# A graph layer's edge loop: two VectorE rows and one ScalarE row of each pair of edge tiles take another place

## The reference, cut to what matters

```python
x_cat = jnp.concatenate([node_feat[src], node_feat[dst], edge_feat], axis=-1)
r = x_cat @ Wr.T + br
q = (node_feat @ Wq.T + bq).reshape(n, H, D)
k = (r @ Wk.T + bk).reshape(e, H, D)
v = (r @ Wv.T + bv).reshape(e, H, D)
a = jnp.einsum('ehd,ehd->eh', q[dst], k) * scaler
amax = jax.ops.segment_max(a, dst, num_segments=n)
ae = jnp.exp(a - amax[dst])
asum = jax.ops.segment_sum(ae, dst, num_segments=n)
m = v * (ae / asum[dst])[..., None]
out = jax.ops.segment_sum(m, dst, num_segments=n).reshape(n, H * D)
```

## Time and profile before

| what | value |
|---|---|
| time, median of 3 runs | 1842.91 us |
| the profiled execution's own time | 1842.91 us |
| its span, first to last instruction | 1841.1 us |
| PE busy | 1623.5 us (88%) |
| DVE busy | 1296.4 us (70%) |
| ACT busy | 1026.3 us (56%) |
| POOL busy | 697.5 us (38%) |

### The profile page before, as it was taken

How to read it: one execution, slowest core, us unless ns; L and a number is a source line. 1 busy time by engine, 2 the same in 40 slices (tenths; PEclk the granted TensorE clock), 3 DMA queues, 4 the chain that set the end, 5 groups by cost and what they waited for, 6 DMA issues and landing times. The chain is left out here.

```text
span 1841.1 us, 26829 instructions
## 1 busy us (share of the span) xinstructions
PE 1623.5 (88%) x7162; PEld 1189.9 (65%) x7162; DVE 1296.4 (70%) x3259; ACT 1026.3 (56%) x3674; POOL 697.5 (38%) x723
## 2 busy tenths in 40 slices
PE   7989979999999999999999999999993777888523
PEld 6867767777777777777777777777772333444311
DVE  5875728887888878887888788878883455322688
ACT  3882225777677777777777767776773344100011
POOL 0001224555555555555555555555551000000033
PEclk9999989999999999999999999999995888999855
DMA  5664327566666666666666666666653324000001
GB/s 181 205 227 154 124 86 238 194 207 212 208 205 201 216 211 207 199 217 212 210 201 212 213 216 199 213 215 201 214 161 130 128 88 137 0 1 0 23 12 44
DMA packets 129670, 300.28 MB, mean 163 GB/s; under 512 B 29088, under 2 KB 50727, under 8 KB 129522
## 3 DMA queue, kind: packets, MB, share of 16 engines
q0 software_dynamic: 63600, 180.17, 29.1%
q1 hardware_dynamic: 60738, 107.59, 19.4%
q10 hardware_dynamic: 5184, 10.81, 1.6%
HBM read 271.40 MB, written 66.58 MB: 184 GB/s over the span
## 5 line engine op out<-in xcount | busy, mean ns | idle before, releaser
L1196 ACT ACTIVATE wv<-vv,expd 128x64 f32<-128x64 f32 x1256 | 316.6, 334 | 2.8
L1208 ACT ACTIVATE old<-old,expd 128x64 f32<-128x64 f32 x1256 | 307.7, 334 | 0.0
L1140 POOL DMA_INDIRECT merge<-new,put_id x157 | 161.1, 1026 | 273.7 <-DVE new L1366 242.1
L1409 PE MATMUL psK<-M_hi,efT_hi 128*128 128x512 f32 x628 | 253.4, 403 | 6.4 <-ACT efT_hi L1166 6.4
L1409 PE MATMUL psV<-M_hi,efT_hi 128*128 128x512 f32 x628 | 255.9, 408 | 0.0
L1410 PE MATMUL psV<-M_lo,efT_hi 128*128 128x512 f32 x628 | 249.7, 398 | 0.0
L1410 PE MATMUL psK<-M_lo,efT_hi 128*128 128x512 f32 x628 | 249.2, 397 | 0.0
L1111 POOL DMA_INDIRECT old<-merge,dst_id x157 | 156.0, 994 | 138.3 <-DMA merge<-new,put_id 112.6
L1111 POOL DMA_INDIRECT kv<-kv_table,src_id x157 | 157.1, 1001 | 72.7 <-issue 47.8
L1182 ACT ACTIVATE expd<-diff 128x32 f32<-128x32 f32 (+1 forms) x79 | 18.1, 229 | 293.9 <-DVE diff L1347 293.9
L1111 POOL DMA_INDIRECT qc<-q_table,dst_id x157 | 155.6, 991 | 53.0 <-issue 46.9
(11 more groups left out here) (271 smaller groups left out, 3404.6 us busy)
## 6 DMA issues: line engine op xcount, KB each, us to landing
efT<-in_ef_turned_dram SPq DMA_DIRECT2D x78, 512.0 KB, 5.0
merge<-empty ACTq DMA_DIRECT2D x4, 2640.0 KB, 9.7
rows<-merge SPq DMA_DIRECT2D x40, 264.0 KB, 3.7
row_block<-dst_rows POOLq DMA_DIRECT2D x13, 768.0 KB, 5.8
dst_line<-dst_rows SPq DMA_DIRECT2D x78, 128.0 KB, 2.7
end_line<-end_rows SPq DMA_DIRECT2D x78, 128.0 KB, 4.1
kv_table<-kv_out SPq DMA_DIRECT2D x10, 512.0 KB, 3.2
raw<-in_L_gnn_Wr_dram SPq DMA_DIRECT2D x12, 256.0 KB, 5.1
```

The lines of the kernel that those rows point to most:

```text
L1140: pool.indirect_dma_start(out=merge[2 * (p % 2) + u][:, :], out_offset=bass.IndirectOffsetOnAxis(ap=put_id[:, t:t + 1], axis=0), in_=new[p ...
L1196: act.activation(wv[:, u, h * DH:(h + 1) * DH], vv[p % 2][:, u, h * DH:(h + 1) * DH], ACT.Copy, scale=expd[p % 2][:, u, 0, h:h + 1]).then_ ...
L1208: act.activation(rows, rows, ACT.Copy, scale=expd[p % 2][:, u, 1, h:h + 1]).then_inc(old_scaled, 1)
L1409: pe.matmul(out[:, :], efT_hi[b][:, u, c, :], Me_hi[:, c, col:col + D], start=c == 0, stop=False)
```

## The change

ACT: the rounding of the weights (`exp_hi`) was issued as the last step of a round, behind `weigh_v`. It now stands right behind the exponential. DVE: `exp_lo` and the first `wv_lo` stood behind the scan. They now stand between the two `vv`. The second `wv_lo` stood between the scores of the two tiles and now stands ahead of both. No instruction is added or taken out.

```diff
@@ scalar: weights(p) @@
                 act.activation(expd[p % 2][:, 0:n, :, :], diff[p % 2][:, 0:n, :, :], ACT.Exp, scale=SCALE).then_inc(exp_ready, 1)
-
-            def weights_high(p):
-                n = tiles_of(p)
                 act.wait_ge(exp_ready, exp_at(p))
                 act.activation(exp_hi[p % 2][:, 0:n, :], expd[p % 2][:, 0:n, 0, :], ACT.Copy).then_inc(exp_ready, 1)
...
                     copy_runs(p - 1)
                     weights(p - 1)
                     weigh_v(2 * p - 2)
-                    weights_high(p - 1)
@@ vector: the loop @@
                 if last:
                     add_v(2 * p - 2)
+                if older:
+                    exp_low_part(p - 2)
+                    wv_low_part(2 * p - 4)
                 if last and tiles_of(p - 1) == 2:
                     add_v(2 * p - 1)
                 if last:
                     row_one_hots(p - 1)
                     scan(p - 1)
-                if older:
-                    exp_low_part(p - 2)
-                    wv_low_part(2 * p - 4)
-                if here:
-                    scores(2 * p)
                 if older and tiles_of(p - 2) == 2:
                     wv_low_part(2 * p - 3)
-                if here and tiles_of(p) == 2:
-                    scores(2 * p + 1)
+                if here:
+                    for t in range(2 * p, 2 * p + tiles_of(p)):
+                        add_k(t)
+                        times_q(t)
+                        sum_scores(t)
```

More of the change, by code:

```diff
@@ L1277, in sum_scores @@
                 dve.tensor_reduce(score[p % 2][:, u, :], kq[:, u, :, :], AX.X, ALU.add).then_inc(score_step, 1)
[L1279 to L1282, removed]
             def split_scores(p):
```

## The result

The changed kernel takes 1856.57 us (median of 12 runs, 1849.52 to 1870.13) against 1842.82 us (12 runs, 1840.38 to 1845.91). The ratio is 1.0083, 95% interval 1.0060 to 1.0104: 14 us slower. The forecast was 1843.9 us, with 0.80 on no difference. Its runs also spread more: 21 us from lowest to highest where the kernel before has 6. The profiled execution took 1861.11 us, somewhat more than the median, with a span of 1859.4 us, 18.3 more than before. In the edge loop, from the first `expd` to the last, it takes 1122.1 us instead of 1105.9, 16.2 us more.

The account below looks back on a forecast made before the run. The prediction took ACT and DVE, handing tiles to each other in 14.21 us a pair, as the bound. 1842.91 us plus 75 full pairs x 0 plus 1.0 for the loop's ends gave 1843.9 us, range 1840.5 to 1849.

Parts of the forecast that it names:

- What bounds the kernel: Edge loop: ACT and DVE, handing tiles to each other, set the 14.21 us of a pair; PE does not.
- The ring: Edge loop: ACT's 10.31 us from expd to runs_hi, then 3.90 us through DVE to the next expd, 14.21 us.
- ACT, 0 us: ACT's stretch from expd to runs_hi: stays 10.31 us with exp_hi moved behind expd, change 0 us.
- Rival 3: ACT: exp_hi hides behind expd, -0.10 us x 75 pairs = -7.5 us, 1835 to 1836 us; chance 0.06.
- DVE's list, 0.12 us of cover: DVE's queue behind the second wv_hi: reaches runs_lo 0.12 us before runs_hi releases it, so the period stays 14.21 us.
- Rival 1: DVE: its new list misses the cover and is 0.12 us late, x 75 = +9 us, 1853 us; chance 0.12.
- Transfers ... That leaves 1.8 us for the new neighbour ... I take 0: DMA loads: efT leaves about 3.2 us later beside old, which still lands 1.8 us before DVE needs it; cost 0.
- Rival 2: Fetch of old: served behind efT, it lands 1.4 us late, x 75 = +105 us, 1948 us; chance 0.02.
- The range: Whole kernel time, for 8 in 10: 1840.5 to 1849 us.
- The ends of the loop, + 1.0 us: Last pairs: +0.3 us in the fourth from the end, +0.7 us in the one-tile pair behind it.

Follow-up runs that it names:

- the run made to check it: Changed kernel with the one-hot matrices ahead of the first wv_lo and efT_lo ahead of runs_lo: 1833.64 us, ratio 0.9941 to the kernel before.

## Why the prediction was wrong

- **What bounds the kernel: right.** The ring of ACT's 10.31 us and DVE's 3.90 us is the period. Shortening DVE's part took 35 us off, to PE's 13.76 us a pair.
- **ACT, 0 us: right.** The run with ScalarE's part alone shows no difference. Rival 3 is ruled out.
- **DVE's list, 0.12 us of cover: right**, to 0.02 us, by the timeline and by the run made to check it. Rival 1, to which 0.12 was given, did not happen. The rule of the Trainium skill that spoke for it ("VectorE: DVE Perf Modes", "The DRAIN you can't avoid") does not come out of this trace as a start at the end of the one in front: the spacings from start to start held, 0.60 to 0.61 us for instructions of 0.68. The same section adds that a next instruction that is not held starts earlier, which the prediction left out and with which the trace agrees.
- **"Transfers ... That leaves 1.8 us for the new neighbour ... I take 0": this is the step that failed.** I took `old`'s 3.7 us as given although the change moved 776 KB (lines and features) into its time, and weighed `efT` as the only neighbour. The landing went to 6.6 us. POOL did get to `old` sooner, as I wrote, by 1.3 us at the median, and that pays for a part: 2.9 us longer less 1.3 is 1.6 us of the 1.8 gone, with a spread (5.2 to 8.8 us) that takes the rest in a third of the pairs. Rival 2 had the right place and was given 0.02. Its price was wrong the other way: 105 us for 1.4 us in each pair, where the profile lists 14.9 us in 24 pairs.
- **The range** ended at 1849 because rival 2 stood at the end of a scale that knew only "in time" or "always late". A landing that comes within its own spread of the moment it is needed makes some pairs late, and the time in between should have had most of rival 2's chance.
- **The ends of the loop, + 1.0 us: not borne out, and too small to matter.** From `expd` to `expd` the fourth pair from the end grew from 13.25 to 13.71 us, where + 0.3 was forecast. The one-tile pair took 11.97 us instead of 14.19, not 0.7 more, since PE kept its pace there. That this comes from the change is not shown (last section).

## What to carry to other kernels

When an instruction is moved, follow what it releases on the queues: two one-hot matrices and a scan that nothing on the compute side was late for held SyncE's 776 KB back by some 3 us. A load's time to landing is not a constant of the load (3.7, 4.7 and 6.6 us here for the same rows, by what SyncE loaded beside them), so take the busy share of those engines stretch by stretch, before and after, and compare the slack with the landing's spread rather than with its median. And an engine's free time is worth using only if what fills it leaves the ring, as `efT_lo` did; filling it with work that was outside the ring gains nothing.

## What the runs showed that I had not expected

TensorE's granted clock near the end of the loop. Before, PE stood for 1.59 us ahead of 1380.36 and the stretches from there were granted 0.50 and 0.52, the lower level of 1.2 GHz. In the changed kernel PE stood longer, 2.06 us ahead of the turn, and kept the full clock:
```profile
1380.30:1382.00 1.70, 1.64 (x5) 1.47 (x6) 0.00 (x0) 1.70 (x9) 0.82 (x1) 0.50 0.64 186
1382.00:1387.00 5.00, 5.00 (x14) 3.86 (x14) 1.99 (x8) 1.24 (x6) 0.89 (x1) 0.52 0.12 45
```
```profile
1399.30:1401.20 1.90, 1.72 (x10) 1.50 (x11) 1.78 (x3) 1.90 (x10) 0.94 (x1) 1.00 0.62 158
1401.20:1404.00 2.80, 2.80 (x13) 2.26 (x12) 1.60 (x8) 2.04 (x10) 0.00 (x0) 1.00 0.25 86
```
The twelve products of the last value tile took 5.1 us at the lower level and 2.8 us at the upper one.

The new order is not shown to be the reason. In the run with ScalarE's part alone VectorE's list and PE's waits at this place are those of the kernel before, 0.23 us ahead of the first tile's sums and 1.59 us ahead of the second's, and yet the clock stayed up and the one-tile pair took 11.98 us:
```profile
1384.01 0.24 PE L1470 MATMUL psO<-exp_hi,same 128*128 128x8 f32 x1 [1.59 <-ACT wv_hi L1201]
```
```profile
1383.40:1385.40 2.00, 1.39 (x7) 1.25 (x8) 0.51 (x1) 2.00 (x10) 0.64 (x1) 1.00 0.74 194
```
The run with the features late did the same (11.99 us), and the one with SyncE late did not (14.14 us). So the same work behind the same waits was granted either level, and up to 2.2 us at the loop's end can differ from run to run for this reason alone.
